# A selective-scan kernel: units of 32 channels by 4 states in place of 8 by 16, with shared broadcast tiles

## The chip, the cores and the metric

One core of a Trainium2 chip runs the whole program in one launch. The metric is the device time in microseconds, the median over several runs. All arithmetic in the stage that changes is float32.

## The reference, cut to what matters

The input x is 4 batches of 1024 rows of 128 values. Four blocks follow one another, each on a layer-normed copy of x and added to x: a sparse attention with 16 heads, a feed-forward net with sign weights, a Mamba block, and the same feed-forward net again. The change is inside the Mamba block's scan:

```python
def step(h, inp):
    dt_t, B_t, C_t, u_t = inp                  # (b,256) (b,16) (b,16) (b,256)
    dA = jnp.exp(dt_t[..., None] * A)          # A is (256 channels, 16 states)
    h = dA * h + (dt_t * u_t)[..., None] * B_t[:, None, :]
    y_t = jnp.einsum('ben,bn->be', h, C_t)     # sum over the 16 states
    return (h, y_t)
```

So there are 256 channels times 16 states = 4096 recurrences for each batch, each of 1024 steps, and the states of a channel are summed at the end. dt and dt*u depend on the channel alone, B and C on the state alone.

## The kernel before, in words

Every engine has one queue, written out in a fixed order. `timetable()` (line 460) sorts all steps of the program by a number from the table `PLACES` (line 188), and each engine emits its own steps in that order; the suffix of a step's name tells the engine: `_t` TensorE, `_v` VectorE (DVE), `_s` ScalarE (ACT), `_p` GpSimd (POOL), `_d` the sync engine (SP) that issues the DMAs. Attention, both feed-forward passes and Mamba of different batches are interleaved through these numbers, and semaphores carry the dependencies.

The Mamba block goes through 8 halves m (4 batches of 2 pieces of 512 time steps). For each half, `dt_t`, `dt_s`, `dt_v`, `dt_p`, `dr_v` and `du_p` make dt and dt*u for two blocks of 128 channels, `dt_d` and `du_d` write them to DRAM (`dtd`, `dud`), and `mx_d` writes B and C to DRAM (`bcd`) and reads them back, broadcast over partitions, into `BR` and `CR`. Then come 32 **units** for each half, 256 in all. A unit is one tile of 128 partitions by 512 time steps: 16 states by 8 channels. For unit u:

- `dt8_d` and `du8_d` (lines 688, 694) read 8 rows of dt and of dt*u from DRAM, each repeated over 16 groups of partitions, into one of 6 tiles `DT` and one of 12 tiles `D` (256 KB each). The first 4 units take theirs from TensorE instead (`bdt_t`, `bdu_t`).
- `decay_s` (line 1604) writes exp(A*dt) into PSUM bank 0 or 1.
- `drive_v` (line 1279) or `drive_p` (line 1780) multiplies `D` by B in place. The DVE form reads B from PSUM bank 3 (`PB`), where `bp_s` (line 1594) has copied it once in each half. POOL does 9 of 32 units.
- `scan_v` (line 1293) runs the recurrence with one scan instruction, in place in `D`.
- `out_p` (line 1787) multiplies two units by C on POOL.
- `csum_t(k)` (line 968) takes the four units 4k to 4k+3. Those are four different groups of channels q, so each of its four float32 products writes another 32 partitions of the PSUM bank, `bank[32*q:32*q+32]`. The stationary operand, a slice of `csel`, puts 8 channels into their place among 32, and four successive csum_t fill the 128 channels of a block.

Then `yev_v`, `gate_p`, `mout_t` and `mout_v` finish the half. `warm_t` (line 1021) multiplies an identity matrix by itself (float32, 128 columns) into a free bank; its results are never read. There are 35 such steps with 238 products.

Of the kernel before, what the change touches and what calls it, by code (L numbers as in the profile page):

```python
# [11 lines left out]
ALU = mybir.AluOpType  # L12
# [11 lines left out]
for _name, _n in (("ident", 128), ("qmask", 4), ("csel", 56), ("one8", 1), ("rmask", 2), ("spread", 128)):  # L24
    CONST[_name] = (NCONST, _n)
    NCONST += _n
# [5 lines left out]
def constants():  # L32
    out = np.zeros((128, NCONST), np.float32)

    def put(name, a):
        at, n = CONST[name]
        out[: a.shape[0], at:at + n] = a.reshape(a.shape[0], n)

    p = np.arange(128)
    put("ident", np.eye(128, dtype=np.float32))  # L40
    put("qmask", ((p[:, None] // 8 % 4 == np.arange(4)[None, :]) * float(HD) ** -0.5).astype(np.float32))
    put("csel", (np.arange(56)[None, :] == 24 + p[:, None] % 8).astype(np.float32))
    put("rmask", (p[:, None] // 32 % 2 == np.arange(2)[None, :]).astype(np.float32))
# [49 lines left out]
def channels(r):  # L93

    return r // 16, r % 4, r % 16 // 4

DRIVEN_P = [0, 1, 5, 9, 13, 17, 21, 25, 29]


FIRST = 4


def driver(u):

    return "v" if u < FIRST or u % NR not in DRIVEN_P else "p"

# [28 lines left out]
def shared_to(i):  # L137
# [17 lines left out]
FOURS = [(k,) for k in range(NCORE // 4)]  # L155
STEPS = [
    (HALVES, 'bp_s mln_p mln_s mln_t mln_v mno_s mxu_s mx_d mx_s mx_t mz_s mz_t silu_s'),
    (BLOCKS, 'dr_v dt_d dt_p dt_s dt_t dt_v du_d du_p mu_s mu_t'),
    (CORE, 'decay_s scan_v'),
    (CORE[FIRST:], 'dt8_d du8_d'),  # L160
    (CORE[:FIRST], 'bdt_t bdu_t'),
# [39 lines left out]
    "aown_s": [22888, 23365, 25999, 30715, 30887, 40479, 40651, 40823, 49274, 49385, 52214, 52325, 52635, 52746, 52857, 52968, 65711,
# [5 lines left out]
    "apv_t": [22392, 22869, 25503, 30006, 30390, 37863, 38151, 38439, 48321, 48590, 50167, 50436, 50705, 51726, 51995, 52385, 65235, 65504,  # L207
# [5 lines left out]
    "aqk_s": [12599, 13460, 83745, 90933, 217686, 229368, 391552, 397472],  # L213
    "aqk_t": [10683, 12402, 82687, 86252, 216628, 227988, 390494, 396414],
    "aqm_s": [95867, 108069, 109666, 115602, 143930, 149556, 182112, 196085, 236320, 240099, 250963, 285938, 290195, 313423, 320816,
        349032, 399702, 407203, 436851, 453724, 455321, 465863, 522069, 536973],
    "aqm_v": [15100, 16147, 19958, 25966, 27356, 34290, 50156, 51203],
    "asb_t": [18781, 20093, 26101, 33215, 36792, 42398, 45716, 46694, 57271, 58249, 64164, 81709, 103956, 116398, 126925, 151769, 152732,
        171471, 176848, 182247, 191047, 196027, 202015, 215650, 244770, 263734, 275330, 300637, 308980, 314158, 328711, 335721, 349851,
        356743, 361307, 365387, 412039, 432125, 450801, 468186, 470238, 491060, 497713, 508092, 527851, 541580, 565666, 587183],  # L220
    "asc_s": [19940, 20434, 21252, 26171, 27260, 30221, 34736, 35230, 37951, 38445, 43557, 44051, 46875, 47369, 47863, 49496, 58430, 58924,
# [5 lines left out]
    "asc_t": [15017, 17376, 23722, 30781, 34178, 38830, 40614, 43376, 53786, 55014, 61954, 69897, 99357, 114093, 124005, 148047, 149452,  # L227
# [1650 lines left out]
```

## Time and profile before

| | |
|---|---|
| median of 3 runs | 813.26 us (810.76 to 814.96) |
| the profiled execution | 808.2 us, span 806.4 us |
| mean granted TensorE clock | 0.976 |
| PE busy | 729.3 us, 90% |
| DVE busy | 690.0 us, 86% |
| ACT busy | 613.8 us, 76% |
| POOL busy | 598.2 us, 74% |
| DMA | 152.93 MB, 70.4% of the 16 engines' span |

Busy time is the union of the intervals in which an engine executed something, so instructions that overlap are counted once. PE is TensorE's products and PEld its weight loads. A float32 product appears as two records, a 16-bit one as one. The records of successive products overlap, so the distance between two starts says more than a mean duration.

### The profile page before, as it was taken

The numbers are of one execution on the slowest core, as the hardware profiler recorded it, in microseconds if no ns is written. First come the engines' busy times: TensorE is split into PE (matmuls) and PEld (weight loads), VectorE is DVE, ScalarE is ACT, GpSimd is POOL, SyncE is SP. The second block draws the span as 40 slices with busy tenths as digits, with TensorE's granted clock in tenths as the row PEclk, the third lists the DMA queues.
The fourth block names the chain that finished last, engine by engine and source line by source line (L and its number), as shares of the span: only waits on it lengthen the run. The fifth ranks groups of instructions, "written<-read, shape, count | busy, mean of one in ns | idle before, by whom it ended". The sixth has DMA issues, their size and how long they took to land. (4 is left out here: it accounts for less than half of the span.)

```text
span 806.4 us, 22760 instructions
## 1 busy us (share of the span) xinstructions
PE 729.3 (90%) x8284; PEld 441.3 (55%) x8284; DVE 690.0 (86%) x1147; ACT 613.8 (76%) x1227; POOL 598.2 (74%) x589
## 2 busy tenths in 40 slices
PE   6989996998789999999899989979998999788888
PEld 5666653644455446556465366546555555354557
DVE  6878146999999999998899899999998989889963
ACT  4767686899779999998699988888669557656423
POOL 3023254878898998879797798889989989898751
PEclk9999998999999999999999999989999999799999
DMA  6000017798879769877768898979798999799940
GB/s 205 3 3 2 2 57 171 204 232 235 200 210 238 198 190 237 231 220 199 188 201 219 216 251 235 254 204 264 222 246 213 237 259 239 211 284 232 229 118 28
DMA packets 83025, 152.93 MB, mean 190 GB/s; under 512 B 9305, under 2 KB 9954, under 8 KB 82914
## 3 DMA queue, kind: packets, MB, share of 16 engines
q1 hardware_dynamic: 82914, 151.48, 70.4%
q8 instruction: 66, 1.08, 0.6%
q14 instruction: 45, 0.37, 0.2%
HBM read 140.43 MB, written 11.01 MB: 188 GB/s over the span
## 5 line engine op out<-in xcount | busy, mean ns | idle before, releaser
L1798 POOL TENSOR_TENSOR d<-d,cr 128x1024 f32<-128x1024 f32 x128 | 300.4, 2355 | 27.0 <-DVE d L1303 17.3
L1620 ACT ACTIVATE ps<-dt,An 128x512 f32<-128x512 f32 x252 | 170.7, 691 | 59.9 <-DVE d L1303 43.1
L1303 DVE TENSOR_TENSOR_SCAN d<-ps,hl,d 128x512 f32<-128x512 f32 x128 | 157.8, 1266 | 4.4 <-ACT ps L1620 2.6
L1303 DVE TENSOR_TENSOR_SCAN d<-ps,d 128x512 f32<-128x512 f32 x128 | 150.5, 1206 | 6.5 <-ACT ps L1620 4.9
L892 PE MATMUL ps<-h,w 128*128 128x512 f16 (+1 forms) x512 | 118.0, 382 | 7.3 <-DVE h L1238 6.7
L1291 DVE TENSOR_TENSOR d<-ps,d 128x512 f32<-128x512 f32 x182 | 117.3, 671 | 5.9 <-DMA d<-dud 5.9
L1785 POOL TENSOR_TENSOR d<-d,br 128x512 f32<-128x512 f32 x70 | 88.8, 1275 | 19.9 <-DMA d<-dud 16.1
L892 PEld LDWEIGHTS ps<-h,w 128*128 128x128 f16 x512 | 47.6, 99 | 80.9 <-DVE h L1238 17.5
L981 PE MATMUL ps<-d,cst 128*32 128x512 f32 x512 | 69.6, 619 | 7.7 <-POOL d L1798 7.2
L1028 PEld LDWEIGHTS ps<-cst 128*128 128x128 f32 x476 | 59.4, 200 | 18.2 <-issue 10.2
L1028 PE MATMUL ps<-cst 128*128 128x128 f32 x476 | 63.4, 287 | 5.3 <-DMA cst<-in_w 5.3
L903 PEld LDWEIGHTS ps<-w,h 128*128 128x128 f32 x496 | 58.5, 193 | 8.4 <-issue 5.3
L1457 ACT COPY pt<-ps 128x512 f32<-128x512 f32 x96 | 52.9, 590 | 11.9 <-PE ps L830 8.2
L903 PE MATMUL ps<-w,h 128*128 128x128 f32 x496 | 60.4, 278 | 0.9 <-ACT h L1516 0.7
L830 PE MATMUL ps<-cst,sx 128*128 128x128 f32 x384 | 55.5, 279 | 6.3 <-ACT sx L1450 2.4
L932 PE MATMUL ps<-xnT,Wk 128*128 128x512 f32 x128 | 57.6, 596 | 0.5 <-ACT xnT L1548 0.2
L830 PEld LDWEIGHTS ps<-cst,sx 128*128 128x128 f32 x384 | 42.1, 141 | 24.8 <-issue 9.4
L847 PEld LDWEIGHTS ps<-v,pt 128*32 128x32 f32 x3072 | 33.9, 111 | 34.5 <-issue 33.1
L847 PE MATMUL ps<-v,pt 128*32 128x18 f32 (+1 forms) x3072 | 39.2, 192 | 11.7 <-issue 6.7
L1164 DVE TENSOR_REDUCE mn<-ps 128x8 f32<-128x512 f32 x64 | 41.3, 678 | 5.1 <-PE ps L807 4.9
L1450 ACT ACTIVATE sx<-ps 128x512 f32<-128x512 f32 x48 | 28.4, 591 | 21.3 <-PE ps L821 21.0
L1238 DVE SCALAR_TENSOR_TENSOR h<-ps,h 128x512 f16<-128x512 f32 (+1 forms) x64 | 39.4, 662 | 6.0 <-ACT h L1510 5.8
(183 smaller groups left out, 1368.8 us busy)
## 6 DMA issues: line engine op xcount, KB each, us to landing
d<-dud SPq DMA_DIRECT2D x252, 256.0 KB, 5.1
dt<-dtd SPq DMA_DIRECT2D x252, 256.0 KB, 5.6
dud<-sE SPq DMA_DIRECT2D x16, 256.0 KB, 4.5
dtd<-sR SPq DMA_DIRECT2D x16, 256.0 KB, 3.9
X<-in_x SPq DMA_DIRECT2D x8, 256.0 KB, 6.2
br<-bcd SPq DMA_DIRECT2D x8, 256.0 KB, 3.3
cr<-bcd SPq DMA_DIRECT2D x8, 256.0 KB, 3.7
out<-X SPq DMA_DIRECT2D x3, 512.0 KB, 5.6
```

The lines of the kernel that those rows point to most:

```text
L830: t = eng.transpose(bank[:, 128 * k:128 * k + 128], sx[:, 128 * k:128 * k + 128], ident)
L847: t = eng.matmul(bo[32 * j:32 * j + 32, at, a, :], pt[:, i, 32 * j:32 * j + 32], V[:, 2 * kk + w, :, 4 * (2 * c + a) + j, :], start=True, ...
L892: t = eng.matmul(bank[:, 0:N], w1[:, ki, 128 * mo:128 * mo + 128], h0[:, s, ki, 0:N], start=(ki == s == 0), stop=(ki == 3 and s == 1))
L903: t = eng.matmul(bank_of["fl3", i][:, 128 * k:128 * k + 128], h1[:, mo, 128 * k:128 * k + 128], w2[:, mo, :], start=(mo == k == 0), stop=( ...
L932: t = eng.matmul(bank[:, :], Wk[:, k, 128 * eb:128 * eb + 128], xnT[:, 1 + k:513 + k], start=(k == 0), stop=(k == KC - 1))
L981: t = eng.matmul(bank[32 * q:32 * q + 32, :], csel[:, 24 - 8 * w:56 - 8 * w], D[:, (4 * k + q) % ND, :], start=(w == 0), stop=(w == 3))
L1028: eng.matmul(banks[k][:, 0:128], ident, ident, start=True, stop=True)
L1291: eng.tensor_tensor(d, PB[:, :], d, ALU.mult).then_inc(v_dr, 1)
L1303: eng.tensor_tensor_scan(d, banks[u % NG][:, :], d, hl[:, r:r + 1] if m % 2 else 0.0, ALU.mult, ALU.add).then_inc(v_sc, 1)
L1620: eng.activation(banks[u % NG][:, :], src[:, :], ACT.Exp, scale=An[:, g:g + 1]).then_inc(s_da, 1)
L1785: eng.tensor_tensor(d, d, BR[m % 2][:, :], ALU.mult).then_inc(p_dr, 1)
L1798: eng.tensor_tensor(d, d, CR[m % 2][:, :].unsqueeze(1).to_broadcast((128, n, 512)), ALU.mult).then_inc(p_cm, n)
```

## The change

A unit now holds 4 states (w) by 32 channels. The four units 4k to 4k+3 are the same 32 channels q with the four groups of states. Therefore:

- One broadcast tile of dt and one of dt*u serve four units: `dt4_d` and `du4_d` load 62 tiles each (before: 252 each) into 2 tiles `DT` and 2 tiles `DU`. The first 8 units (`SPREAD` = 2 fours) take theirs from TensorE, with 2 `bdt_t` and 2 `bdu_t` (before 4 and 4).
- B and C now differ between the units of a four, so `BR` and `CR` are 4 tiles each, loaded by `br_d` and `cr_d`: 32 loads each (before 8 each).
- What stands in PSUM bank 3 is dt*u and no longer B: `bp_s(k)` copies it once for each four, 62 copies (before 8), and waits for the DVE drives before it. `drive_v` multiplies it by `BR[:, w]` into `D`, which is now written there for the first time.
- `D` has 10 tiles (before 12). POOL drives 8 of 32 units (before 9): 62 in all (before 70), and DVE 194 (before 186).
- `csum_t(k)` has its four products accumulate over w into one and the same group of 32 partitions.
- `warm_t` multiplies `e4` (bfloat16) with itself, repeated to 512 columns: 26 steps with 199 products; one step of 8 float32 products stays as `wake_t`.
- The tables `PLACES` and `WARM` have new numbers throughout.

```diff
-DRIVEN_P = [0, 1, 5, 9, 13, 17, 21, 25, 29]
-FIRST = 4
+SPREAD = 2
+DRIVEN_P = [0, 4, 8, 12, 16, 20, 24, 28]
...
 PLACES = {
...
-    "bdt_t": [111521, 113193, 117361, 121885],
...
 WARM = [
-    (8848, 2, 8), (10191, 0, 3), (102142, 5, 5), (108670, 7, 6), (111520, 2, 7), (197534, 4, 1), (203846, 6, 3), (212706, 2, 3),
...
+    (8848, 2, 8), (10191, 0, 3), (108900, 7, 3), (111706, 5, 10), (129102, 7, 3), (179854, 7, 3), (246380, 5, 5), (269152, 7, 9),
...
-        ND = 12
+        ND = 10
...
-        NT = 6
+        NT, NQ = 2, 2
         DT = sb("dt", [128, NT, 512])
-        BR = [sb(f"br{i}", [128, 512]) for i in range(2)]
-        CR = [sb(f"cr{i}", [128, 512]) for i in range(2)]
+        DU = sb("du", [128, NQ, 512])
+        BR, CR = (sb(n, [128, 4, 512]) for n in ("br", "cr"))
...
+            def br_d(m, w):
+                u = NR * m - 4 + w
+                eng.wait_ge(l_bc, 16 * (m + 1))
+                if m and driver(u) == "v":
+                    eng.wait_ge(v_dr, driven(u + 1, "v"))
+                elif m:
+                    eng.wait_ge(p_dr, driven(u + 1, "p"))
+                eng.dma_start(BR[:, w, :], states(m, 4 * w)).then_inc(l_b[w], 16)
...
-                e = 128 * eb + 32 * q + 8 * w
-                return src[m % 2][e:e + 8, :].unsqueeze(0).to_broadcast((16, 8, 512))
+                e = 128 * eb + 32 * q
+                return src[m % 2][e:e + 32, :].unsqueeze(0).to_broadcast((4, 32, 512))
...
+            def du4_d(k):
+                if k >= NQ + SPREAD:
+                    eng.wait_ge(s_bp, k - NQ - SPREAD + 1)
+                    eng.wait_ge(p_dr, driven(4 * (k - NQ) + 4, "p"))
+                eng.wait_ge(l_du, 16 * (k // 4 + 1))
+                eng.dma_start(DU[:, k % NQ, :], rows(dud, k)).then_inc(l_q[k % NQ], 16)
...
             def csum_t(k):
 
-                m, eb, w = k // 8, k // 4 % 2, k % 4
-                if w == 0:
+                m, eb, q = k // 8, k // 4 % 2, k % 4
+                if q == 0:
                     bank_of["y", m, eb] = PY.turn(eng, (v_yg, 2 * m + eb + 1))
...
-                for q in range(4):
-                    t = eng.matmul(bank[32 * q:32 * q + 32, :], csel[:, 24 - 8 * w:56 - 8 * w], D[:, (4 * k + q) % ND, :],
+                for w in range(4):
+                    t = eng.matmul(bank[32 * q:32 * q + 32, :], spread[:, 0:32], D[:, (4 * k + w) % ND, :],
                                    start=(w == 0), stop=(w == 3))
                 t.then_inc(t_y, 1)
...
             def warm_t(k, products):
 
                 for s, v in emptied.get(k, ()):
                     eng.wait_ge(s, v)
-                eng.wait_ge(l_w1, 16)
+                eng.wait_ge(v_set, V_SEL)
                 for _ in range(products):
-                    eng.matmul(banks[k][:, 0:128], ident, ident, start=True, stop=True)
+                    eng.matmul(banks[k][:, :].rearrange("p (a n) -> p a n", a=4), e4[:, :], e4[:, :].unsqueeze(1).to_broadcast((128, 4, 128)), start=True, stop=True)
...
             def drive_v(u):
-                m = u // NR
-                d = D[:, u % ND, :]
...
-                eng.wait_ge(s_bp, m + 1)
-                eng.wait_ge(l_d[u % ND], 16 * landed(u, ND))
-                eng.tensor_tensor(d, PB[:, :], d, ALU.mult).then_inc(v_dr, 1)
+                else:
+                    eng.wait_ge(t_y, (u - ND) // 4 + 1)
+                eng.wait_ge(l_b[w], 16 * (m + 1))
+                if k < SPREAD:
+                    eng.wait_ge(t_bdu, k + 1)
+                else:
+                    eng.wait_ge(s_bp, k - SPREAD + 1)
+                eng.tensor_tensor(D[:, u % ND, :], PB[:, :], BR[:, w, :], ALU.mult).then_inc(v_dr, 1)
...
-            def bp_s(m):
+            def bp_s(k):
...
-                eng.wait_ge(l_br, 32 * (m + 1))
-                eng.copy(PB[:, :], BR[m % 2][:, :]).then_inc(s_bp, 1)
+                eng.wait_ge(v_dr, driven(4 * k, "v"))
+                eng.wait_ge(l_q[k % NQ], 16 * landed(k, NQ))
+                eng.copy(PB[:, :], DU[:, k % NQ, :]).then_inc(s_bp, 1)
```

The queue of TensorE around the sums, in the middle of the program where one half's scans run beside another batch's attention. Before (L981 is `csum_t`, L1028 `warm_t`, L932 `mu_t`, L942 `mx_t`, L922 `mz_t`):

```order
L830 MATMUL ps<-cst,sx 128x128 x4
L932 MATMUL ps<-xnT,Wk 128x512 x4
L779 MATMUL ps<-masks,e 128x512 x2
L807 MATMUL ps<-KD,qm 128x2x64 x8
L981 MATMUL ps<-d,cst 32x512 x4
L1028 MATMUL ps<-cst 128x128 x7
L942 MATMUL ps<-u,wgt 41x512 x2
```

With the change, at a like place (L975 is `csum_t`, L1027 `warm_t`, L922 `mu_t`, L932 `mx_t`):

```order
L792 MATMUL ps<-KD,qm 64x2x32 x32
L932 MATMUL ps<-u,wgt 41x512 x2
L811 MATMUL ps<-zf,cst 128x512
L942 MATMUL ps<-lnm,Wdt 128x512
L975 MATMUL ps<-d,cst 32x512 x4
L1027 MATMUL ps<-e 128x512 x6
L820 MATMUL ps<-cst,sx 128x128 x8
L882 MATMUL ps<-h,w 128x512 x32
L837 MATMUL ps<-v,pt 32x4x9 x32
L975 MATMUL ps<-d,cst 32x512 x4
```

The sums stand among the same kinds of steps as before and are still four products each. Only the partitions that they write differ, which a row of the order does not show.

The queue of ScalarE at the start of a half, beside a batch's feed-forward pass. Before (L1620 is `decay_s`):

```order
L1620 ACTIVATE ps<-dt,An 128x512
L1525 ACTIVATE lnm<-X,mr 128x128 x4
L1436 COPY v<-ps 64x4x16x8 x2
L1545 COPY xnT<-xnT 128x4
L1548 ACTIVATE xnT<-ps,wgt 128x512
L1450 ACTIVATE sx<-ps 128x512
L1620 ACTIVATE ps<-dt,An 128x512
L1493 ACTIVATE lnf<-X,frs 128x128 x4
L1557 COPY zs<-ps 128x512 x2
L1620 ACTIVATE ps<-dt,An 128x512
```

With the change (L1615 is `decay_s`, L1598 the copy `bp_s`):

```order
L1598 COPY ps<-du 128x512
L1525 ACTIVATE lnm<-X,mr 128x128 x4
L1436 COPY v<-ps 64x4x16x8 x2
L1545 COPY xnT<-xnT 128x4
L1548 ACTIVATE xnT<-ps,wgt 128x512
L1615 ACTIVATE ps<-dt,An 128x512
L1450 ACTIVATE sx<-ps 128x512
L1450 ACTIVATE sx<-sx 128x512
L1534 ACTIVATE X<-X,mr 128x128 x4
L1615 ACTIVATE ps<-dt,An 128x512 x2
L1557 COPY zs<-ps 128x512 x2
L1598 COPY ps<-du 128x512
```

Two copies of `bp_s` now stand among the decays of this piece, where before there was none; the steps of the other stages are the same kinds in almost the same order.

## Rows read from the trace of the kernel before

**Rows 1.** Page, part 1: busy us, share of the span, instructions.

```profile
PE 729.3 (90%) x8284; PEld 441.3 (55%) x8284; DVE 690.0 (86%) x1147; ACT 613.8 (76%) x1227; POOL 598.2 (74%) x589
```

**Rows 2.** Three stretches: length, busy of PE, PEld, DVE, ACT, POOL, clock, DMA, GB/s.

```profile
0.00:140.00 140.00, 122.77 (x1970) 81.53 (x1970) 85.08 (x238) 95.86 (x212) 45.30 (x87) 0.98 0.22 64
140.00:740.00 600.00, 550.54 (x5907) 319.70 (x5908) 561.13 (x847) 490.42 (x961) 518.05 (x478) 0.98 0.85 225
740.00:806.00 66.00, 55.97 (x409) 40.04 (x407) 43.77 (x64) 27.53 (x56) 34.83 (x26) 0.97 0.54 137
```

**Rows 3.** The middle stretch, line 981 alone (PE, PEld).

```profile
140.00:740.00 600.00, 63.19 (x464) 9.77 (x464) 0.98 0.85 225
```

**Rows 4.** Groups of TensorE: count, busy us, mean ns, idle before and releaser.

```profile
L981 PE MATMUL ps<-d,cst 128*32 128x512 f32 x512 | 69.6, 619 | 7.7 <-POOL d L1798 7.2 <-DVE d L1324 0.2 <-DVE u L1310 0.2
L981 PEld LDWEIGHTS ps<-d,cst 128*32 128x32 f32 x512 | 10.7, 109 | 27.7 <-issue 14.3 <-POOL d L1798 11.2 <-DVE u L1310 0.3
L932 PE MATMUL ps<-xnT,Wk 128*128 128x512 f32 x128 | 57.6, 596 | 0.5 <-ACT xnT L1548 0.2 <-issue 0.2
L932 PEld LDWEIGHTS ps<-xnT,Wk 128*128 128x128 f32 x128 | 23.6, 189 | 28.5 <-issue 27.3 <-ACT xnT L1548 0.9
L892 PE MATMUL ps<-h,w 128*128 128x512 f16 (+1 forms) x512 | 118.0, 382 | 7.3 <-DVE h L1238 6.7 <-DVE sR L1277 0.6
L1028 PE MATMUL ps<-cst 128*128 128x128 f32 x476 | 63.4, 287 | 5.3 <-DMA cst<-in_w 5.3
```

**Rows 5.** Timeline of PE: start us, duration of the run of instructions, line, count.

```profile
504.63 3.60 PE L932 MATMUL ps<-xnT,Wk 128*128 128x512 f32 x8
508.17 0.39 PE L779 MATMUL ps<-masks,e 64*128 64x512 bf16 x2
509.39 1.06 PE L981 MATMUL ps<-d,cst 128*32 128x512 f32 x8
510.39 1.83 PE L1028 MATMUL ps<-cst 128*128 128x128 f32 x14
512.37 1.88 PE L942 MATMUL ps<-u,wgt 128*41 128x512 f32 x4 [0.15 <-ACT u L1569]
```

**Rows 6.** Two stretches of 5 us, PE alone: busy, granted clock.

```profile
520.00:525.00 5.00, 3.30 (x17) 1.00 0.85 234
525.00:530.00 5.00, 2.09 (x19) 0.59 0.74 187
```

**Rows 7.** Groups of DVE, POOL and ACT in the scan.

```profile
L1291 DVE TENSOR_TENSOR d<-ps,d 128x512 f32<-128x512 f32 x182 | 117.3, 671 | 5.9 <-DMA d<-dud 5.9
L1303 DVE TENSOR_TENSOR_SCAN d<-ps,d 128x512 f32<-128x512 f32 x128 | 150.5, 1206 | 6.5 <-ACT ps L1620 4.9 <-POOL d L1785 0.5
L1785 POOL TENSOR_TENSOR d<-d,br 128x512 f32<-128x512 f32 x70 | 88.8, 1275 | 19.9 <-DMA d<-dud 16.1 <-DVE d L1303 3.8
L1798 POOL TENSOR_TENSOR d<-d,cr 128x1024 f32<-128x1024 f32 x128 | 300.4, 2355 | 27.0 <-DVE d L1303 17.3
L1602 ACT COPY ps<-br 128x512 f32<-128x512 f32 x8 | 4.6, 578 | 0.0
```

**Rows 8.** Waits on transfers: us in total, times, longest.

```profile
ACT ps L1620 <- DMA dt<-dtd: 16.3, 10, 6.7
POOL d L1785 <- DMA d<-dud: 16.1, 12, 4.2
```

**Rows 9.** DMA issues: count, KB each, median us to landing.

```profile
d<-dud SPq DMA_DIRECT2D x252, 256.0 KB, 5.1
dt<-dtd SPq DMA_DIRECT2D x252, 256.0 KB, 5.6
br<-bcd SPq DMA_DIRECT2D x8, 256.0 KB, 3.3
```

**Rows 10.** The chain that ended last: start us, us, what.

```profile
782.05 1.10 PE ps L981 x8
```

More of the change, by code:

```diff
@@ L23 @@
 CONST, NCONST = {}, 0
-for _name, _n in (("ident", 128), ("qmask", 4), ("csel", 56), ("one8", 1), ("rmask", 2), ("spread", 128)):
+for _name, _n in (("ident", 128), ("qmask", 4), ("one8", 1), ("rmask", 2), ("spread", 128)):
     CONST[_name] = (NCONST, _n)
@@ L41, in constants @@
     put("qmask", ((p[:, None] // 8 % 4 == np.arange(4)[None, :]) * float(HD) ** -0.5).astype(np.float32))
-    put("csel", (np.arange(56)[None, :] == 24 + p[:, None] % 8).astype(np.float32))
     put("rmask", (p[:, None] // 32 % 2 == np.arange(2)[None, :]).astype(np.float32))
-    put("spread", (p[:, None] % 32 == p[None, :] % 8).astype(np.float32))
+    put("spread", (p[:, None] % 32 == p[None, :] % 32).astype(np.float32))
     put("one8", (p == RK).astype(np.float32))
@@ L90, with landed @@
 NCORE = NM * NR
-def channels(r):
-    return r // 16, r % 4, r % 16 // 4
-DRIVEN_P = [0, 1, 5, 9, 13, 17, 21, 25, 29]
-FIRST = 4
+SPREAD = 2
+DRIVEN_P = [0, 4, 8, 12, 16, 20, 24, 28]
 def driver(u):
-    return "v" if u < FIRST or u % NR not in DRIVEN_P else "p"
+    return "v" if u < 4 * SPREAD or u % NR not in DRIVEN_P else "p"
 def driven(u, by):
     return sum(driver(x) == by for x in range(u))
-def landed(u, n):
-    return u // n + 1 - (u % n < FIRST)
+def landed(k, n):
+    return sum(x % n == k % n for x in range(SPREAD, k + 1))
 def rows_of(f):
@@ L214 @@
[L214 to L220, printed above, removed]
@@ new lines @@
+    "cr_d": [113611, 114226, 114841, 115456, 202771, 203386, 204001, 204616, 278128, 278743, 279374, 279989, 368833, 369448, 370063,
+        378025, 449633, 450248, 452055, 452670, 534357, 534972, 537022, 537637, 605941, 606556, 608256, 608871, 675538, 676153, 678203,
+        678818],
+    "csum_t": [125491, 146676, 150974, 167022, 171458, 183808, 192781, 200074, 214445, 221512, 234883, 243512, 257975, 264997, 274743,
[4 rows of a table added]
+    "decay_s": [115586, 116199, 119115, 119847, 122377, 122990, 125372, 125985, 137788, 138401, 139970, 141061, 143250, 144861, 145508,
[16 rows of a table added]
@@ new lines @@
+    "jsum_p": [53142, 99982, 202745, 255690, 356486, 375140, 519100, 594907],
+    "jtr_v": [58834, 105674, 210327, 261382, 367118, 382673, 531768, 603352],
+    "jx_v": [60945, 108097, 214062, 265543, 372514, 392193, 535370, 605703],
+    "lg_v": [739023, 739365],
+    "lm_t": [739507, 739954],
+    "lm_v": [740151, 741331],
+    "lmo_t": [734776, 735967],
+    "lpre_p": [705112],
+    "mln_p": [83973, 148057, 241856, 294675, 412103, 465847, 562089, 633560],
+    "mln_s": [88566, 156042, 246815, 300371, 417087, 471700, 566918, 637931],
@@ L448 @@
+    "store_d": [497300, 620288, 724614, 745040, 756211, 759851],
+    "vz_p": [10085],
+    "yev_v": [169436, 202106, 257145, 288429, 331615, 373122, 426145, 457262, 498221, 540759, 579213, 611401, 649975, 680800, 714265],
 }
 WARM = [
[5 rows of a table removed]
[4 rows of a table added]
 ]
 def timetable():
-    rows = [(at, "warm_t", (k, products)) for at, k, products in WARM]
+    rows = [(at, "warm_t" if i else "wake_t", (k, products)) for i, (at, k, products) in enumerate(WARM)]
     for whom, names in STEPS:
@@ L489, in const @@
             return cst[0:rows, at:at + n]
-        ident, qmask, csel, one8, rmask, spread = (const(n) for n in ("ident", "qmask", "csel", "one8", "rmask", "spread"))
+        ident, qmask, one8, rmask, spread = (const(n) for n in ("ident", "qmask", "one8", "rmask", "spread"))
         masks = sb("masks", [128, 288], BF16)
@@ L952, in dt_t, with bdt_t, bdu_t @@
                 eng.matmul(bank[:, :], Wdt[0:9, 128 * eb:128 * eb + 128], xS[0:9, :], start=True, stop=True).then_inc(t_md, 1)
-            def bdt_t(u):
-                bank = bank_of["bdt", u] = turn((s_da, u + 1))
+            def bdt_t(k):
+                bank = bank_of["bdt", k] = turn((s_da, 4 * k + 4))
                 eng.wait_ge(v_md, 2)
-                q = slice(32 * u, 32 * u + 32)
+                q = slice(32 * k, 32 * k + 32)
                 eng.matmul(bank[:, :], spread[q, :], sR[q, :], start=True, stop=True).then_inc(t_bdt, 1)
-            def bdu_t(u):
-                bank = bank_of["bdu", u] = turn((v_dr, u + 1))
+            def bdu_t(k):
+                if k == 0:
+                    for sm, v in emptied.get(3, ()):
+                        eng.wait_ge(sm, v)
+                else:
+                    eng.wait_ge(v_dr, driven(4 * k, "v"))
                 eng.wait_ge(p_md, 3)
-                q = slice(32 * u, 32 * u + 32)
-                eng.matmul(bank[:, :], spread[q, :], sE[q, :], start=True, stop=True).then_inc(t_bdu, 1)
+                q = slice(32 * k, 32 * k + 32)
+                eng.matmul(PB[:, :], spread[q, :], sE[q, :], start=True, stop=True).then_inc(t_bdu, 1)
             def csum_t(k):
-                m, eb, w = k // 8, k // 4 % 2, k % 4
-                if w == 0:
+                m, eb, q = k // 8, k // 4 % 2, k % 4
+                if q == 0:
                     bank_of["y", m, eb] = PY.turn(eng, (v_yg, 2 * m + eb + 1))
@@ L1019, in lm_t, with wake_t @@
                 t.then_inc(t_mo, 1)
+            def wake_t(k, products):
+                eng.wait_ge(l_w1, 16)
+                for _ in range(products):
+                    eng.matmul(banks[k][:, 0:128], ident, ident, start=True, stop=True)
             def warm_t(k, products):
@@ L1791, in out_p @@
                 d = D[:, u % ND:u % ND + n, :]
-                if r == 0:
-                    eng.wait_ge(l_br, 32 * (m + 1))
+                for w in range(u % 4, u % 4 + n):
+                    eng.wait_ge(l_c[w], 16 * (m + 1))
                 eng.wait_ge(v_sc, u + n)
```

285 lines of the change are left out of this document (137 added, 148 removed), and 296 rows, old and new, of tables (PLACES, WARM).

## The prediction

> **What bounds the kernel now.** I read the page's first part, then the busy time by stretches, then the groups of instructions, then TensorE's timeline. The first part shows TensorE at 729.3 us of a span of 806.4, DVE at 690.0, ACT at 613.8, POOL at 598.2 [rows 1]. A share over the whole span hides stages, so three stretches follow [rows 2]. The sums run from 142 to 782 us, so the middle one, 140 to 740, is the scan. There TensorE is busy 550.54 of 600 us (92%), DVE 561.13 (94%), POOL 518.05, ACT 490.42. TensorE and DVE are both nearly full and each now and then waits for the other; what is added to one of them in full beside no relief of that same engine must show in the time. In the middle TensorE has 49.5 us of idle time left, and 63.4 us of its whole busy time are the idle products of line 1028, which nobody needs [rows 4]. That is all its room: 77 us idle plus 63 us of filler.
>
> **The change, part by part.**
>
> *The sums.* Every csum_t has four float32 products of 512 columns, 64 times. Before, the four write four different groups of 32 partitions. The timeline shows one such step starting at 509.39 and the next work at 510.39: four products in 1.00 us [rows 5]. All 64 keep TensorE busy for 69.6 us, 1.09 each, where 512 records of 619 ns laid end to end would be 317 us [rows 4]: the four run at the same time, side by side. With the change all four write the same group of 32 partitions, bank[32q : 32q+32], and accumulate there. The nearest row for products that follow one another into the same partitions is line 932, four float32 products of 512 columns into one bank: started at 504.63, next work at 508.17, so 3.54 us [rows 5]. That row has 128 columns of weights. Line 942 shows that few columns don't help when the products share them: two products 41 columns wide into one place take 1.88 us, 0.94 each [rows 5]. So a sum goes from 1.00 to 3.54 us, 2.54 us more, and 64 of them add 162.6 us. The bounds: nothing, if the four still ran side by side, and 4 x 0.94 = 3.76 us (174 us in all) by line 942. I take 3.54. In the middle stretch lie 464 of the 512 records [rows 3], 58 sums, so 147 us of it come there, three times the idle time of that stretch. This is what decides.
>
> A rule of the Trainium skill would make this dearer. The trace first: line 932 has 128 loads of 189 ns, one ahead of each record, and its eight records still start 3.54 / 8 = 443 ns apart, so the loads are hidden behind the products [rows 4, 5]. The page "TensorE: Matmul & The Clock Gate", Part 3 (packing small matmuls), says that a weight load overlaps running products only when it goes to another group of rows; here all sums use all rows. By it each of the eight loads would stand bare, and this is the third rival below; by the row they cost nothing, and the sum goes by the row.
>
> *The idle products.* Out go 63.4 us (238 products). In come 8 of the old form, 8 x 63.4/238 = 2.1 us, and 199 16-bit products of 512 columns. The nearest row is line 892, 118.0 us / 512 = 0.230 us each [rows 4], so 45.9 us. Together 15.4 us less. They no longer fill gaps if TensorE has none: whatever stands in its queue counts in full.
>
> *The products that spread the first units.* 4 instead of 8, at 57.6 / 64 = 0.90 us [rows 4]: 3.6 us less.
>
> *DVE.* 194 drives instead of 186: 8 x 0.671 = 5.4 us more, on 690.0 [rows 7]. The scans stay. Its 5.9 us of waits for tiles of dt*u may go [rows 7].
>
> *ACT.* 62 copies into bank 3 instead of 8, 54 x 0.578 = 31.2 us more [rows 7], to 645. Each is now a link: the last drive of a four, the copy, the next drive. At 0.58 us plus the way there and back it fits beside a scan of 1.2 us if a scan stands between them in DVE's queue; 62 times bare it would be 36 us of DVE. The load of dt*u behind it takes 5.1 us to land [rows 9], with 2 tiles ahead, against four units of at least 4 x (1.21 + 0.67) = 7.5 us [rows 7]. Hidden.
>
> *POOL.* 8 drives fewer at 1.275: 10.2 us less [rows 7].
>
> *Transfers.* 504 loads of 256 KB become 124; those of B and C go from 16 to 64 [rows 9]. In all 520 become 188, and 85% busy DMA engines in the middle stretch [rows 2] become about a third of that. It ends the waits of 16.3 us on ACT and 16.1 us on POOL [rows 8]. But no engine with a wait on a transfer is the one that will bound, so I count nothing. The loads of B for a half may start when the unit four places earlier has used the tile; 3.3 us to landing [rows 9] against the same 7.5 us: hidden.
>
> *The sum.* TensorE busy: 729.3 + 162.6 - 15.4 - 3.6 = 872.9 us, more than the whole span now. Per 600 us of the middle the others need at most 561 + 5, so there TensorE alone is the bound, and what stood idle in it is mostly used. I keep the idle time of the start (140 - 122.77 = 17 us), 8 us of the last stretch (10 now), where the chain passes through the last sum and the last feed-forward pass [rows 2, 10], and 3% of some 700 us in the middle, 21 us: 8.2% is idle there now with DVE as full as TensorE, and DVE will be at about 80%. Together 46 us, so 918.9. Against that stands the clock. In the one 5 us stretch of [rows 6] TensorE is busy 2.09 us after a stretch with 3.30, and its granted clock is 0.59 of full speed, so partly at the lower level; its mean over the middle is 0.98 [rows 2]. Fewer gaps should give back part of the 2.4% of 806 us, 19 us, that this costs; I take 8. The span comes to 911 us, and with the 1.8 us by which the profiled execution stands over its span, 913. The profiled execution of before (808.2) is 5.1 us under the median of the runs (813.3). An after that is bound by TensorE may spread less, so I add 2: **915 us**, 12.5% more than 813.3.
>
> **The rivals.**
>
> 1. *The products still run side by side, or TensorE hides them: faster.* If sharing the partitions did not serialise them, the price of the sums is zero, and the relief decides: up to 15.4 + 3.6 us of TensorE where it bounds, and the transfers' waits of 5.9 to 16.3 us on the other three. Half of either counts as each bounds half the time: 813 - 10 - 8 = 795 us. For it: the products do not depend on one another except through the accumulator. Against: lines 932 and 942 are just such products, and run at 0.89 to 0.94 us each. The point from which it decides is a sum under about 1.3 us: 64 x 0.3 is what the fillers give back. Chance 0.05. An outcome within 0.5% of before, which is about what a measurement of this kernel can tell, needs a chance meeting between the two: 0.02.
> 2. *The queues slip against one another.* D has 10 tiles in place of 12, and the drives of units 4k+10 and 4k+11 wait for sum k, 2.5 us later than now. Two such units must be driven, scanned, multiplied by C and summed before sum k+2: 2 x 0.67 + 2 x 1.21 + 2.36 = 6.1 us of work in a row [rows 7], against two sums every 24 us (700 / 58 each 12). That fits, but behind a waiting drive in DVE's fixed order stand the steps that TensorE needs next, and behind the copy to bank 3 stand ACT's. Then TensorE would keep its 77 us of idle time, and 872.9 + 77 - 3 gives 947 us; with half of the bare 36 us of copies 965. Chance 0.14.
> 3. *The weights are loaded in the open.* 8 x 0.109 us per sum [rows 4], x 64 = 56 us more: 971 us. Line 932 speaks against it. Chance 0.05.
> 4. *TensorE has more room than its busy time tells.* Ends of products are modelled, and a run of products counts its last one to the end: 1.09 us instead of 1.00 for a sum. If some 5% of 729 us is such tails, the true need is 36 us lower and the time about 878. Chance 0.12.
>
> **How the numbers follow.** The forecast itself, TensorE bound with sums of about 3.5 us, gets 0.62 and spans 890 to 940: from idle time of 20 to 70 us. Rival 4 reaches below to 870, rival 2 above to 965. I take 872 to 955: it leaves out the faster and the same case (0.07), most of rival 3 (0.05) and a part of rivals 2 and 4. Slower by over 0.5%: 0.62 + 0.14 + 0.05 + 0.12 = 0.93; faster 0.05; the same 0.02.
>
> **What would show it right or wrong.** The group of the sums has 512 records as before and is busy not for 69.6 but for about 228 us, 3.6 for each run of eight. TensorE's share of the span goes to 93% or more, DVE's falls to about 76%, POOL's to 65%. Waits of DVE's drives and of ACT behind TensorE's sums appear, where now waits for transfers stand; DMA falls to some 60 MB. The idle products take 48 us. The forecast fails if a run of eight records lasts about 1.1 us (rival 1), or 4.4 us (rival 3), or if TensorE still idles 70 us or more in the middle (rival 2).

## The result and the profile after

The changed kernel takes 973.11 us (median of 4 runs, 972.02 to 976.38), the one before 813.59 us in the same comparison. The ratio is 1.197, with a 95% interval of 1.193 to 1.202. The forecast of 915 us had the sign and the bound right and the size too small; 973 lies above its range of 872 to 955. The ratios here and below use the runs of the faster of two states only; of all the runs behind them four stood in the slower one, at a granted clock of 0.576 to 0.942 (1417 us of b_serial, the longest, among them).

The page of the changed kernel, its first part, the sum of the transfers and the sync engine's queue:

```profile
PE 872.9 (90%) x8015; PEld 447.1 (46%) x8015; DVE 700.3 (72%) x1155; ACT 644.6 (66%) x1281; POOL 589.8 (61%) x581
...
DMA packets 32954, 65.77 MB, mean 68 GB/s; under 512 B 1737, under 2 KB 2386, under 8 KB 32850
...
q1 hardware_dynamic: 32850, 64.39, 18.3%
```

TensorE's busy time is 872.9 us after 729.3 [rows 1], to the tenth what the prediction summed. Its idle time is 972.2 - 872.9 = 99.3 us, where 46 were forecast. DVE, ACT and POOL are all further from full than before. The transfers fell from 152.93 to 65.77 MB.

The same by stretches (columns as in [rows 2]; the sums now run from 141 to 948 us):

```profile
0.00:140.00 140.00, 119.55 (x1930) 77.08 (x1930) 87.64 (x239) 96.30 (x210) 43.66 (x81) 0.96 0.15 53
140.00:905.00 765.00, 691.50 (x5748) 336.04 (x5749) 572.35 (x856) 520.50 (x1014) 514.46 (x478) 0.97 0.20 73
905.00:972.00 67.00, 61.89 (x338) 34.02 (x336) 40.32 (x62) 27.83 (x58) 31.64 (x24) 1.00 0.10 36
```

The middle has 73.5 us of idle time on TensorE, more than the 49.5 of before, though TensorE had far more to do. The groups of line 975 (the sums), 1027 (16-bit idle products), 1290 and 1783 (the drives on DVE and POOL), to be held against [rows 4, 7]:

```profile
L975 PE MATMUL ps<-d,cst 128*32 128x512 f32 x512 | 231.6, 611 | 9.9 <-POOL d L1796 9.8
L1027 PE MATMUL ps<-e 128*128 128x512 bf16 x199 | 47.3, 380 | 0.0
L1290 DVE TENSOR_TENSOR d<-ps,br 128x512 f32<-128x512 f32 x194 | 127.7, 677 | 82.8 <-PE ps L975 45.4 <-DMA br<-bcd 15.8 <-ACT ps L1598 11.4
L1783 POOL TENSOR_TENSOR d<-du,br 128x512 f32<-128x512 f32 x62 | 78.7, 1272 | 80.1 <-PE ps L975 48.9 <-DMA du<-dud 31.2
```

The sums went from 69.6 to 231.6 us, 228 being forecast. The timeline shows one of them alone, with the step behind it: 3.55 us from start to start.

```profile
405.26 3.62 PE L975 MATMUL ps<-d,cst 128*32 128x512 f32 x8
408.81 1.53 PE L820 MATMUL ps<-cst,sx 128*128 128x128 f32 x12
```

The last two groups show what was not forecast: DVE's and POOL's drives, with 5.9 and 19.9 us of idle time ahead of them before [rows 7], now have 82.8 and 80.1 us. The waits that end there, and the others on transfers, from the view of waits (total us, times, longest):

```profile
POOL d L1783 <- PE ps L975: 48.9, 14, 12.8
DVE d L1290 <- PE ps L975: 45.4, 24, 3.5
POOL d L1783 <- DMA du<-dud: 31.2, 15, 4.8
ACT ps L1598 <- DMA du<-dud: 31.0, 9, 5.0
POOL hl L1794 <- DMA cr<-bcd: 27.2, 5, 11.2
ACT ps L1615 <- DMA dt<-dtd: 17.1, 6, 9.1
DVE d L1290 <- DMA br<-bcd: 15.8, 7, 3.8
```

The first two are waits for the sums, since a drive needs a tile of `D` back. The other five are waits for transfers, 136 us in total on three engines with the 14.0 us that out_p itself waits for C; before, the largest two were 16 us each [rows 8] and DVE's came to 5.9 [rows 7]. There are 188 of these loads where there were 520, and they are waited for far more. The windows of 3 us around the change of a half, DMA engines alone (clock, DMA share, GB/s):

```profile
343.00:346.00 3.00, 1.00 0.26 102
349.00:352.00 3.00, 1.00 0.26 102
355.00:358.00 3.00, 1.00 0.26 102
```

The issue of the loads of C (L658) and, in the kernel before, of dt*u (L701): minimum, median, maximum in ns.

```profile
L658 SPq DMA_DIRECT2D cr<-bcd x32: 500/1052/5052, 119.2 to 863.2; - x32
L701 SPq DMA_DIRECT2D d<-dud x252: 514/549/1457, 120.7 to 773.2; - x126
```

SP's queue at the same place issues three loads of B and four of C one after another (start, us until the last is issued), 16 us in all:

```profile
338.23 5.34 SPq L652 DMA_DIRECT2D br<-bcd  x3
343.67 10.54 SPq L658 DMA_DIRECT2D cr<-bcd  x4
```

From 339 to 360 us, while these loads are in flight, the rate stands at 101 to 103 GB/s and the share at 0.26 to 0.27. In the middle stretch before, it was 225 GB/s at 0.85 [rows 2]. At 102 GB/s one load of 256 KB needs 2.57 us. An issue lasted up to 5.05 us, where none of the loads of dt*u before took over 1.46, so the queue and all that stood behind in it was held back. The chain of waits through the same place shows what that does to TensorE:

```profile
338.83 2.23 SPq L652
341.17 2.41 SPq L652
344.79 16.28 DMA cr<-bcd
...
361.30 0.20 POOL hl L1794
...
369.59 3.75 PE ps L987 x16
```

The timeline of TensorE at that step:

```profile
369.59 3.75 PE L987 MATMUL ps<-w,u 128*128 128x128 f32 x16 [8.33 <-POOL u L1802]
```

The load of C takes 16 us, POOL waits for it with `out_p`, behind that in POOL's queue stands the gating of the last half, and line 987, the output projection on TensorE, starts at 369.6. TensorE sat idle for 8.3 us ahead of it. This is the worst place. At the seven changes of a half POOL waits for C 4.4, 10.0, 0, 3.2, 2.3, 0.3 and 7.4 us, and 13.7 us before the first half.

### The profile page after: what moved, and what is told of

Same layout as the page of the kernel before. It is cut to its first block, busy times and chain, and to the rows that moved or that the text cites. A ratio compares the mean times of both kernels' runs of the same rounds, so it can differ in the third digit from the quotient of the medians.

```text
span 972.2 us, 21795 instructions
## 1 busy us (share of the span) xinstructions
PE 872.9 (90%) x8015; PEld 447.1 (46%) x8015; DVE 700.3 (72%) x1155; ACT 644.6 (66%) x1281; POOL 589.8 (61%) x581
## 2 busy tenths in 40 slices
DMA packets 32954, 65.77 MB, mean 68 GB/s; under 512 B 1737, under 2 KB 2386, under 8 KB 32850
## 4 chain that ended last, share of the span: by engine, by line
PE 57%; DMA 16%; issue 6%; DVE 6%; POOL 6%; ACT 5%; SPq 4%; POOLq 0%; DVEq 0%; ACTq 0%
PE ps L975 17%; PE ps L882 7%; PE ps L922 6%; DMA du<-dud 5%; DMA cr<-bcd 5%; DMA br<-bcd 4%; PE ps L893 4%; PE ps L811 3%; PE ps L820 3%; POOL d L1796 2%; PE ps L837 2%; PE ps L871 2%; SPq L658 2%; DMA dt<-dtd 2%; PE ps L797 2%
## 5 line engine op out<-in xcount | busy, mean ns | idle before, releaser
L975 PE MATMUL ps<-d,cst 128*32 128x512 f32 x512 | 231.6, 611 | 9.9 <-POOL d L1796 9.8
L1615 ACT ACTIVATE ps<-dt,An 128x512 f32<-128x512 f32 x248 | 168.0, 690 | 67.8 <-DVE d L1302 50.4
L1290 DVE TENSOR_TENSOR d<-ps,br 128x512 f32<-128x512 f32 x194 | 127.7, 677 | 82.8 <-PE ps L975 45.4
L1783 POOL TENSOR_TENSOR d<-du,br 128x512 f32<-128x512 f32 x62 | 78.7, 1272 | 80.1 <-PE ps L975 48.9
L975 PEld LDWEIGHTS ps<-d,cst 128*32 128x32 f32 x512 | 51.1, 112 | 160.7 <-issue 154.0
L882 PE MATMUL ps<-h,w 128*128 128x512 f16 (+1 forms) x512 | 113.8, 373 | 6.8 <-DVE h L1237 5.4
L1598 ACT COPY ps<-du 128x512 f32<-128x512 f32 x62 | 36.5, 589 | 42.6 <-DMA du<-dud 31.0
L922 PE MATMUL ps<-xnT,Wk 128*128 128x512 f32 x128 | 56.8, 592 | 0.5 <-issue 0.5
L837 PE MATMUL ps<-v,pt 128*32 128x18 f32 (+1 forms) x3072 | 42.9, 194 | 9.0 <-issue 3.4
L837 PEld LDWEIGHTS ps<-v,pt 128*32 128x32 f32 x3072 | 36.6, 113 | 27.6 <-issue 26.6
L1794 POOL TENSOR_SCALAR hl<-d 128x2 f32<-128x2 f32 x64 | 12.4, 193 | 60.6 <-DVE d L1302 33.0
```

Source lines behind the costliest of these rows:

```text
L837: t = eng.matmul(bo[32 * j:32 * j + 32, at, a, :], pt[:, i, 32 * j:32 * j + 32], V[:, 2 * kk + w, :, 4 * (2 * c + a) + j, :], start=True, ...
L882: t = eng.matmul(bank[:, 0:N], w1[:, ki, 128 * mo:128 * mo + 128], h0[:, s, ki, 0:N], start=(ki == s == 0), stop=(ki == 3 and s == 1))
L922: t = eng.matmul(bank[:, :], Wk[:, k, 128 * eb:128 * eb + 128], xnT[:, 1 + k:513 + k], start=(k == 0), stop=(k == KC - 1))
L975: t = eng.matmul(bank[32 * q:32 * q + 32, :], spread[:, 0:32], D[:, (4 * k + w) % ND, :], start=(w == 0), stop=(w == 3))
L1290: eng.tensor_tensor(D[:, u % ND, :], PB[:, :], BR[:, w, :], ALU.mult).then_inc(v_dr, 1)
L1615: eng.activation(banks[u % NG][:, :], src[:, :], ACT.Exp, scale=An[:, g:g + 1]).then_inc(s_da, 1)
```

## The experiments

Twelve kernels ran, each beside the kernel before on the same chip. Two theories came first. **A**: the serial sums alone make the loss, because TensorE's idle time cannot be used up by them. **B**: they would be worth what was forecast, and the changed buffers and loads cost the rest. Theories C and D came later and stand in the expectation of a_16. The comparisons ran on several chips, and the kernel before took 811.9 to 813.6 us in them, so a difference between kernels of two comparisons can be off by about 2 us.

### The sums alone in the kernel before (b_serial)

```diff
                 for q in range(4):
-                    t = eng.matmul(bank[32 * q:32 * q + 32, :], csel[:, 24 - 8 * w:56 - 8 * w], D[:, (4 * k + q) % ND, :],
-                                   start=(w == 0), stop=(w == 3))
+                    t = eng.matmul(bank[32 * w:32 * w + 32, :], csel[:, 24 - 8 * w:56 - 8 * w], D[:, (4 * k + q) % ND, :],
+                                   start=(q == 0), stop=(q == 3))
```

> The kernel before, its four products of a sum all sent to one group of 32 partitions (they then sum over the wrong units), nothing else changed. Both theories: TensorE busy 729.3 + 162 = 891 us, 3.55 us for a run of eight records. Theory A (the serial sums alone make the loss, because TensorE's idle time can't be used up by them): idle stays near 77 us, span near 968 us. Theory B (the idle time is taken up, and the smaller rings and single tiles of the changed kernel made the rest of the loss): idle falls to about 45 us, span 925 to 938 us.

Measured: 936.61 us, ratio 1.152 (1.145 to 1.159). Its page:

```profile
PE 878.9 (94%) x8284; PEld 479.3 (51%) x8284; DVE 691.8 (74%) x1147; ACT 617.0 (66%) x1227; POOL 598.0 (64%) x589
...
L981 PE MATMUL ps<-d,cst 128*32 128x512 f32 x512 | 231.3, 606 | 5.6 <-POOL d L1798 5.6
```

The group grows to 231.3 us, as in the changed kernel, and the idle time falls to 934.8 - 878.9 = 55.9 us. The loss is 125 us for 162 us of longer sums. By the spans (934.8 and 806.4) it is 128 us: the busy time grew by 149.6 us, 12 less than expected, at a mean granted clock of 0.984 after 0.976, and 21 us went into idle time that had been there. That is the step of the prediction as it was made, on the old buffers, and it fits theory B.

### The sums side by side in the changed kernel (a_spread)

```diff
-                    t = eng.matmul(bank[32 * q:32 * q + 32, :], spread[:, 0:32], D[:, (4 * k + w) % ND, :],
-                                   start=(w == 0), stop=(w == 3))
+                    t = eng.matmul(bank[32 * w:32 * w + 32, :], spread[:, 0:32], D[:, (4 * k + w) % ND, :],
+                                   start=(q == 0), stop=(q == 3))
```

> The changed kernel, the four products of a sum each sent to another group of 32 partitions (they then sum over channel groups and not over states), nothing else changed. Theory A: the loss goes with the serial sums, 973 - 160 = 813 us, perhaps 795 with the cheaper idle products. Theory B: the new couplings cost time of their own, so it stays above 830 us.

Measured: 901.52 us, ratio 1.109 (1.101 to 1.117). The page has TensorE no longer as the bound:

```profile
PE 747.6 (83%) x8015; PEld 420.2 (47%) x8015; DVE 698.3 (78%) x1155; ACT 642.4 (71%) x1281; POOL 588.9 (66%) x581
```

TensorE is idle for 151 us of its span of 898.6, and its mean granted clock is 0.934. So without the serial sums the changed kernel is still 90 us slower than before. Something else in it costs nearly as much.

### Without the reloads of B and C (a_nobc)

`br_d` and `cr_d` return at once for m > 0, and the waits count only the first load of each tile. Left out: 56 of the 64 loads of B and C.

> The changed kernel, its tiles of B and C loaded in the first half only (56 loads of 256 KB and the waits on them left out, so later halves compute with old B and C). Waits on them in the trace were 15.8 us on DVE and 27.2 us on POOL. Theory A: under 10 us faster, 963 to 973. Theory B: 15 to 40 us faster, 933 to 958.

Measured: 922.99 us, ratio 1.136 (1.130 to 1.143), 50 us less than the changed kernel, more than theory B expected. The idle time falls from 99 to 55 us, since the span is 923.8:

```profile
PE 869.0 (94%) x8015; PEld 444.6 (48%) x8015; DVE 699.3 (76%) x1155; ACT 644.1 (70%) x1281; POOL 589.1 (64%) x581
```

So these 56 loads make most of the 58 us that were not foreseen. Two causes remained possible: a tile that is free too late (there is one per group of states), or a load that is slow.

### The same loads with another slowest dimension (a_16)

In the changed kernel the source of every broadcast load has the shape (4, 32, 512), in the kernel before (16, 8, 512). Here it is (32, 4, 512): partition p holds channel p//4 and state p%4. The bytes of the loads, the tiles, the waits and the order of the queues are the same; the constants follow the new order of partitions.

```diff
-                return bcd[m % 2][at:at + 4, :].unsqueeze(1).to_broadcast((4, 32, 512))
+                return bcd[m % 2][at:at + 4, :].unsqueeze(0).to_broadcast((32, 4, 512))
...
-                return src[m % 2][e:e + 32, :].unsqueeze(0).to_broadcast((4, 32, 512))
+                return src[m % 2][e:e + 32, :].unsqueeze(1).to_broadcast((32, 4, 512))
...
-    put("spread", (p[:, None] % 32 == p[None, :] % 32).astype(np.float32))
+    put("spread", (p[:, None] % 32 == p[None, :] // 4).astype(np.float32))
+    put("csel", (p[:, None] // 4 == np.arange(32)[None, :]).astype(np.float32))
...
-    al = a["attn_b_A_log"].reshape(2, 4, 32, 4, 4).transpose(4, 2, 0, 1, 3).reshape(128, 32)
+    al = a["attn_b_A_log"].reshape(2, 4, 32, 4, 4).transpose(2, 4, 0, 1, 3).reshape(128, 32)
```

> The changed kernel, its 188 broadcast loads read in another order: partition p is channel p//4 and state p%4 (before: state p//32, channel p%32), so that the slowest dimension of every load is 32 instead of 4; the constants follow. In the trace of the changed kernel every stretch with such loads waiting shows 102 GB/s and a DMA share of 0.26, and eight loads of B and C in a row hold the queue for 20 us. Theory C (a load whose slowest dimension is 4 runs on 4 of the 16 DMA engines): stretches reach 200 GB/s or more, the issues of the loads of C stop lasting 1 to 5 us, the waits on loads fall from 140 to under 40 us, 912 to 930 us. Theory D (the waits come from single tiles that are free too late, whatever the speed of a load): 955 to 975 us.

Measured: 911.86 us, ratio 1.123 (1.118 to 1.127): 61 us faster than the changed kernel by the order in which the loads go through their source, and theory C. Page, DMA issues (count, KB, median us to landing), the issue of the loads of C in ns, and two windows of 3 us with such loads in flight:

```profile
PE 859.6 (95%) x8015; PEld 441.3 (49%) x8015; DVE 697.2 (77%) x1155; ACT 643.6 (71%) x1281; POOL 588.9 (65%) x581
```

```profile
du<-dud SPq DMA_DIRECT2D x62, 256.0 KB, 3.2
dt<-dtd SPq DMA_DIRECT2D x62, 256.0 KB, 2.9
br<-bcd SPq DMA_DIRECT2D x32, 256.0 KB, 3.4
cr<-bcd SPq DMA_DIRECT2D x32, 256.0 KB, 3.6
```

```profile
L659 SPq DMA_DIRECT2D cr<-bcd x32: 512/554/1629, 118.0 to 802.8; - x32
```

```profile
315.00:318.00 3.00, 1.00 0.87 280
318.00:321.00 3.00, 1.00 0.87 321
```

The loads land in 2.9 to 3.6 us, where the page of the changed kernel could give no landing time for any of the four groups, and the rate reaches 280 and 321 GB/s instead of 102. TensorE is busy 859.6 us and idle 907.3 - 859.6 = 47.7; the prediction had 46. The waits of the drives, and the group of POOL's drives:

```profile
DVE d L1291 <- PE ps L976: 58.6, 32, 4.5
POOL d L1784 <- PE ps L976: 39.6, 14, 10.7
```

```profile
L1784 POOL TENSOR_TENSOR d<-du,br 128x512 f32<-128x512 f32 x62 | 78.6, 1273 | 41.3 <-PE ps L976 39.6 <-DMA du<-dud 1.7
```

The last entry, 1.7 us, is what the trace still shows of the 136 us of waits on these loads, so theory D, in which the single tiles come free too late, is out. DVE and POOL wait 98 us in total for the sums, as much as in the changed kernel. These waits alone do little harm, since TensorE has work meanwhile. Of the 65 us between the spans of the two kernels, 52 are idle time of TensorE and 13 its busy time, with a mean granted clock of 0.992 after 0.968 for the same products.

### Both causes out (a_16_spread)

The edit of a_spread on the kernel of a_16.

> The same, and the four products of a sum each sent to another group of 32 partitions (they then sum over channel groups and not over states). With both causes gone what is left is the rest of the change. Theory C: 800 to 825 us. If single buffers and the copies into bank 3 cost something of their own, 830 to 880 us.

Measured: 790.90 us, ratio 0.975 (0.970 to 0.980), 9 us below the range of theory C. With it the four corners stand:

| | loads with 4 outermost | loads with 32 outermost |
|---|---|---|
| sums in one group | 973.1 | 911.9 |
| sums side by side | 901.5 | 790.9 |

Each cause alone costs 111 us (loads) and 121 us (sums), both together 182 us, about 50 less than their sum. That TensorE works off its long sums while the others wait for a load, or the reverse, would explain it, but no run shows that by itself. The remaining parts of the change, among them 62 copies into bank 3, single tiles of B and C and the ring of 10, are together worth a gain of 21 us.

### The idle products (a_nowarm, a_16_nowarm, b_warm16)

`timetable()` leaves out all of `WARM` but its first step. For b_warm16 the kernel before uses the 16-bit product in its own 34 later steps.

> The changed kernel without its 26 steps of 16-bit idle products (47.3 us of TensorE; the first 8 products stay). If TensorE is the bound where they stand, 973 - 35 = 935 us or less. If they only fill gaps, 968 to 978 us, or more if the clock falls for want of them.

> The kernel of a_16 without its 26 steps of 16-bit idle products. Beside the changed kernel they cost 14 us of their 47, since TensorE had idle time for the rest. With TensorE waiting less, more of them should count: 20 to 40 us under a_16.

> The kernel before, its idle products after the first 8 turned from 230 float32 products of 128 columns into as many 16-bit ones of 512 columns, at the same places. 230 x 0.267 = 61 us of busy time become 230 x 0.236 = 54 us. If they fill gaps, no difference beyond 0.5%; if each counts where it stands, up to 7 us faster.

Measured: 964.38 us for a_nowarm (973.1 with them), 903.73 for a_16_nowarm (911.9 with them), 808.03 for b_warm16, ratio 0.9955 (0.993 to 0.998). The pages of the first two:

```profile
PE 844.4 (88%) x7816; PEld 435.6 (45%) x7816; DVE 699.8 (73%) x1155; ACT 644.8 (67%) x1281; POOL 589.2 (61%) x581
```

```profile
PE 831.2 (92%) x7816; PEld 428.5 (47%) x7816; DVE 697.2 (77%) x1155; ACT 643.8 (71%) x1281; POOL 588.8 (65%) x581
```

Without the products 28 us of busy time go in either kernel, not the 47 to 50 that they take, and the mean granted clock falls from 0.968 to 0.950 and from 0.992 to 0.972. Both expectations missed: a_nowarm is 9 us faster, between its two cases, and a_16_nowarm 8 us, where 20 to 40 were expected from a first figure of 14 us, which was the difference of the two profiled executions of the changed kernel and a_nowarm alone. In b_warm16 the saving is 4 us, just under the half per cent that was set as the bound for a difference; its busy time of 727.5 us is 2 below that of the kernel before, where 7 were expected.

### 16-bit sums: the fastest version (a_16_f16), and its neighbours

Four products that share their partitions can't be run side by side, but each can be shorter. The product with C is written in 16 bits over the first half of its own tile, and the selection matrix `ch` is 16-bit too; the accumulation stays float32. This rounds h*C to float16, which neither kernel does.

```diff
-                    t = eng.matmul(bank[32 * q:32 * q + 32, :], csel[:, :], D[:, (4 * k + w) % ND, :],
+                    t = eng.matmul(bank[32 * q:32 * q + 32, :], ch[:, :], DH[:, (4 * k + w) % ND, 0:512],
...
-                eng.tensor_tensor(d, d, CR[:, u % 4:u % 4 + n, :], ALU.mult).then_inc(p_cm, n)
+                eng.tensor_tensor(DH[:, u % ND:u % ND + n, 0:512], d, CR[:, u % 4:u % 4 + n, :], ALU.mult).then_inc(p_cm, n)
```

> The kernel of a_16 with both causes taken out and the sum over the states kept: the product with C is written in 16 bits into the same tile, and the four products of a sum, still into one group of 32 partitions, multiply it by a 16-bit selection matrix, one record each. A 16-bit product of 512 columns took 0.236 us in the changed kernel's idle products, so a sum is 4 x 0.24 = 0.95 us in place of 3.55, and TensorE's busy time falls by 166 us. By theory C and the price of the serial sums 780 to 795 us, like a_16_spread, and faster than both kernels. If 16-bit output slows POOL's product with C (300 us busy), over 800.

Measured: **787.55 us**, ratio 0.971 (0.966 to 0.975), faster than both kernels and as fast as a_16_spread, which sums over the wrong index. Page and groups:

```profile
PE 716.9 (91%) x7759; PEld 416.5 (53%) x7759; DVE 694.4 (88%) x1155; ACT 640.1 (81%) x1281; POOL 588.4 (75%) x582
```

```profile
L981 PE MATMUL ps<-d,ch 128*32 128x512 f16 x256 | 65.9, 389 | 4.6 <-POOL d L1804 4.4
L1804 POOL TENSOR_TENSOR d<-d,cr 128x1024 f16<-128x1024 f32 x128 | 300.2, 2353 | 23.4 <-DVE d L1308 13.3 <-POOL hl L1802 0.9
```

A sum now takes 65.9 / 64 = 1.03 us, about as much as the four side by side did (69.6 / 64 = 1.09), with half the records. TensorE's busy time fell by 143 us, where 166 were expected, and POOL's product is not slower for its 16-bit output (2353 ns against 2355 in [rows 7]). Three more beside it:

> The changed kernel with the 16-bit sums alone, its loads as they are, four repetitions outermost. The slow loads then stand without the slow sums: a_spread measured 901 us with sums of about 1.1 us each. Theory C: 890 to 905 us, so about 110 us above a_16_f16. If the sums' price came from something else than TensorE's time, 940 us or more.

Measured: 907.81 us, ratio 1.116 (1.110 to 1.122), 120 us over a_16_f16 for the order of the loads alone, and 3 us above what was expected. It agrees with a_spread, whose sums are of the same length by another way, so what the sums cost is their time on TensorE.

> The kernel of a_16_f16 without the 26 steps of idle products. If they hold the clock up in gaps that TensorE has anyway, it is 5 to 25 us slower than with them; if they stand in the way, up to 15 us faster.

Measured: 791.75 us, ratio 0.973 (0.967 to 0.978). The 4 us to a_16_f16 lie within the intervals; whether the idle products help there is not settled.

> The kernel before with 16-bit sums alone: four products side by side, 1.06 us before, go to about 0.4 us. 64 x 0.65 = 42 us less TensorE time where TensorE and DVE bound by turns: 790 to 805 us. If DVE bounds alone, 808 to 813 us.

Measured: 825.47 us, ratio 1.017 (1.011 to 1.022): some 1.7% slower, against both expectations.

```profile
PE 700.5 (85%) x8028; PEld 445.3 (54%) x8028; DVE 692.1 (84%) x1147; ACT 614.0 (75%) x1227; POOL 597.2 (73%) x590
...
L986 PE MATMUL ps<-d,ch 128*32 128x512 f16 x256 | 26.5, 405 | 10.7 <-POOL d L1805 10.5 <-DVE u L1315 0.2
```

The sums shrink from 69.6 to 26.5 us, but TensorE's busy time only from 729.3 to 700.5, so everything else on it takes 14 us longer, and its mean clock is 0.960 where it was 0.976. Idle time grew from 77 to 120 us. Why it grew, and whether the clock fell because of it, was not tested.

## Why the prediction was wrong

**Right: the price of the sums.** Step "the sums", 1.00 to 3.54 us and 162.6 us in all, was measured as 231.6 - 69.6 = 162.0 us. Line 932 was the right row to read, and rival 3 (bare weight loads, 4.4 us) is out: 3.55 us from start to start. The upper bound by line 942 was given as 174 us in all; its own terms, 64 x (3.76 - 1.00), make 177.

**Right: the size of TensorE's busy time; its last digit is luck.** 872.9 us forecast, 872.9 measured. The idle products took 47.3 + 3.7 = 51.0 us where 48.0 were forecast, and the products that spread the first units fell by 1.4 us and not by 3.6. Other products that came out shorter made up for both, and with the quick loads of a_16 the same products took 859.6 us.

**Right, once the loads are quick: the idle time.** 46 us forecast (17 at the start, 21 in the middle, 8 at the end); 47.7 in a_16 (16, 27 and 5), whose 911.9 us stand 3 us from the forecast of 915, and 55.9 in b_serial. In the changed kernel it was 99.3 us, and 73.5 of them lie in the middle.

**Wrong: the step "transfers".** It reads "504 loads of 256 KB become 124 ... 85% busy DMA engines in the middle stretch [rows 2] become about a third of that". The step counts nothing for the transfers, and a load of dt*u with 5.1 us to landing and one of B with 3.3 us are called hidden. The landing times were taken from loads of the same bytes and of another shape, whose slowest dimension was 16 [rows 9]. With 4 there, stretches with such loads in flight moved 102 GB/s at a DMA share of 0.26, where the middle of the kernel before ran at 225 GB/s, and several loads in flight were no quicker than one after another: at one change of a half seven of them took the queue 16 us to issue, and eight at 2.57 us each are 20.6 us of transfer. In the corners above this cost 61 us beside the serial sums. The DMA share in the middle did fall, from 0.85 to 0.20, where about a third was forecast; a low share was the sign of the loss and not of a relief.

The Trainium skill states this: "DMA: Bandwidth & Descriptors", section "Rules for kernel authors", says in its row on using all 16 engines that the slowest dimension sets how many engines a transfer is split over, and that an outermost dimension of c under 16, such as a leading broadcast of c copies, confines it to at most c. The trace agrees: 4 of 16 is 0.25, and 0.26 was measured. It shows only the mean share of the 16, not which of them were busy. The prediction weighed a rule on weight loads and passed over this one, which spoke against the change in so many words.

**Wrong: the clock.** 8 us back were forecast from fewer gaps. There were more gaps, and the mean granted clock stood at 0.968 after 0.976. In a_16, where TensorE idles 47.7 us and not 99.3, it was 0.992 and TensorE's busy time 13 us under that of the changed kernel.

**The rivals.** Rival 3's 971 us stand 2 us from the result, by luck: its sums of 4.4 us took 3.55. Rival 2 (947 to 965) had the right place, idle time of TensorE, by a mechanism that did not decide. Its sign, 70 us or more of it in the middle, did appear (73.5), but it can't tell late tiles from late loads. Its late tiles of `D` do show, as 94 us of waits for the sums, but a_16 has 98 us of the same waits and 48 us of idle time. Rival 1 gave 795 us for sums that cost nothing; the corner where nothing else costs either is 790.9. Its other half, that the waits for transfers go, was what failed. Rival 4, a time of about 878 us, is out: no kernel with the float32 sums in one group and their idle products in place had a median under 911. No rival had a transfer become slower, although every one of the 188 loads had a new shape; that is the case that was missing.

## What to carry to other kernels

Before "fewer bytes" is booked as a relief, look at the shape of the transfers: here those with 4 as their slowest dimension moved 102 GB/s, and the same bytes with 32 up to 321, and a flat rate with a low DMA share while loads are waited for is how the trace shows it. When a change regroups what an accumulation sums, check which of its products still write different partitions: side by side four took 1.0 us, in a row 3.5 us. And an engine whose busy time the change raises above the old span gives a floor, not the time: add what the others' new waits leave idle.

## What the runs showed that was not expected

- Two causes of 111 and 121 us gave 182 together, so undoing one of them in the changed kernel showed 61 or 72 us only. The loads' 111 us, by the spans of a_spread and a_16_spread (898.6 and 788.2), are 84 us of idle time and 26 us of longer busy time, at a mean granted clock of 0.934 and 0.974.
- With 43 us of sums taken from TensorE the kernel before was 1.7% slower (b_f16), with a granted clock of 0.960 after 0.976 and 14 us more for the other products; the cause is open.
- Idle products cost about 8 us where they took 47 to 50 us of TensorE, even with TensorE at 95% busy (a_16 and a_16_nowarm).
- POOL's product of 1024 columns takes the same 2.35 us with a 16-bit as with a 32-bit output.
